# Attention's last two heads projected by token, and the other fourteen heads' sums divided on GpSimd: one change to a two-layer hybrid kernel on one Trainium2 core

## What is computed

```python
x = x + attention(layernorm(x))
# attention, 16 heads of 8 features each
dots = einsum('bhid,bhjd->bhij', q, k) * 8 ** -0.5      # causal mask, ALiBi bias in the second one
attn = softmax(dots, axis=-1)
out  = einsum('bhij,bhjd->bhid', attn, v)               # heads side by side: 128 features
return out @ Wo
```

## Time and profile before

| | |
|---|---|
| median of 3 runs | 2040.76 us (2034.04 to 2040.94) |
| the profiled execution: its time, its span | 2045.5 us, 2043.6 us |
| busy: TensorE, VectorE, ScalarE, GpSimd | 89%, 78%, 58%, 28% of the span |
| mean granted TensorE clock | 0.943 of full |
| first attention: head 15's third chunk copied to `o_sb`, last addition to `x`, start of each | 944.3 us, 988.1 us |
| second attention: the same two | 1939.1 us, 1982.9 us |

### The profile page before, as it was taken

The page is one execution under the profiler, slowest core; times in us unless marked ns, Lnnn a source line. Parts: engine busy times, 40 slices in busy tenths (PEclk is TensorE's granted clock), DMA queues, the critical chain, the costliest instruction groups (busy, mean ns, idle before and its releaser), DMA issues. The chain is left out here.

```text
span 2043.6 us, 47998 instructions
## 1 busy us (share of the span) xinstructions
PE 1823.2 (89%) x18588; PEld 979.6 (48%) x18588; DVE 1584.5 (78%) x3374; ACT 1175.8 (58%) x2363; POOL 563.1 (28%) x528
## 2 busy tenths in 40 slices
PE   6888888999899999998899978888869999999967
PEld 2444454444355555554544434444534555555454
DVE  6899965666889999983555579999568999999545
ACT  4766623222278888885222257755443888888815
POOL 3898920000200000000100048989330000000022
PEclk9999998999699999998799999999887999999969
DMA  5343300310313222211041124443021233322200
GB/s 167 118 140 116 127 1 1 89 51 27 110 31 53 54 56 50 51 27 22 1 81 49 36 63 116 134 122 105 1 73 51 55 56 60 57 56 40 31 4 21
DMA packets 68719, 127.89 MB, mean 63 GB/s; under 512 B 20679, under 2 KB 30932, under 8 KB 67020
## 3 DMA queue, kind: packets, MB, share of 16 engines
q1 hardware_dynamic: 68076, 124.29, 24.4%
q10 hardware_dynamic: 416, 0.54, 0.1%
HBM read 106.17 MB, written 16.84 MB: 60 GB/s over the span
## 5 line engine op out<-in xcount | busy, mean ns | idle before, releaser
L1774 ACT ACTIVATE a_probs<-a_ps_k 128x512 f32<-128x512 f32 (+3 forms) x1280 | 598.6, 546 | 225.1 <-PE a_ps_k L1688 129.9
L1670 PE MATMUL a_ps_q<-a_k_op,a_q_op 84*32 84x512 bf16 (+7 forms) x5120 | 536.3, 366 | 24.7 <-DMA a_k_op<-a_k_parts 9.6
L1834 DVE TENSOR_REDUCE a_maxes<-a_ps_q 128x1 f32<-128x512 f32 x768 | 504.1, 686 | 67.6 <-PE a_ps_q L1670 64.8
L1684 PE MATMUL a_ps_k<-a_q_op,a_k_op 87*32 87x512 bf16 (+7 forms) x5120 | 517.5, 353 | 2.4 <-ACT a_probs L1774 0.8
L1706 PE MATMUL a_ps_o<-a_probs,a_vh 128*32 128x512 f32 (+3 forms) x2752 | 319.3, 509 | 1.1 <-ACT a_probs L1774 0.8
L1670 PEld LDWEIGHTS a_ps_q<-a_k_op,a_q_op 72*32 72x32 bf16 (+1 forms) x5120 | 186.8, 97 | 171.5 <-DVE a_maxes L1834 69.1
L1831 DVE CUSTOM_DVE_ANT_0 a_ps_q<-a_ps_q,all_c_mask_q 128x128 f32<-128x128 f32 (+3 forms) x512 | 248.2, 496 | 4.9 <-PE a_ps_q L1670 3.8
L1684 PEld LDWEIGHTS a_ps_k<-a_q_op,a_k_op 75*32 75x32 bf16 (+1 forms) x5120 | 185.3, 96 | 135.6 <-ACT a_probs L1774 85.1
L1105 ACT ACTIVATE e_silu<-e_psg,all_me_b 128x512 f32<-128x512 f32 x128 | 87.7, 687 | 230.6 <-PE e_psg L1037 230.6
L1914 POOL CAST a_max_parts<-a_neg_max 128x16 bf16<-128x16 f32 x32 | 6.3, 196 | 751.0 <-DVE a_neg_max L1839 751.0
L1188 DVE SCALAR_TENSOR_TENSOR e_mid<-e_psv,all_me_b,e_silu 128x512 f32<-128x512 f32 x128 | 95.7, 749 | 132.2 <-PE e_psv L1039 128.3
(11 more groups left out here) (296 smaller groups left out, 2585.1 us busy)
## 6 DMA issues: line engine op xcount, KB each, us to landing
m0st_c_rows<-m_bc_rows SPq DMA_DIRECT2D x32, 512.0 KB
e_w_rows<-e_comb SPq DMA_DIRECT2D x64, 256.0 KB, 3.3
m1st_c_rows<-m_bc_rows SPq DMA_DIRECT2D x32, 512.0 KB
a_q_op<-a_q_parts SPq DMA_DIRECT2D x30, 288.0 KB
a_k_op<-a_k_parts SPq DMA_DIRECT2D x30, 288.0 KB
a_outputs<-a_o_sb SPq DMA_DIRECT2D x480, 18.0 KB
m0st_b_rows<-m_bc_rows SPq DMA_DIRECT2D x32, 256.0 KB
m1st_b_rows<-m_bc_rows SPq DMA_DIRECT2D x32, 256.0 KB
```

Of the source, the lines that this page charges most:

```text
L1670: last = pe.matmul(ps_q[32 * r:32 * r + 32, use % QB, 0:width], q_op[h % SLOT][0:NR, part(t, r)], k_op[h % SLOT][0:NR, kc * CH:kc * CH + w ...
L1684: last = pe.matmul(ps_k[32 * r:32 * r + 32, b % KB, 0:width], k_op[h % SLOT][:, part(j, r)], q_op[h % SLOT][:, c * CH + first:c * CH + fir ...
L1774: act.activation(probs[:, n % PSLOT, 0:width], ps_k[:, b % KB, 0:width], ACT.Exp).then_inc(exp_done, 1)
L1834: dve.tensor_reduce(found, bank, AX.X, ALU.max).then_inc(q_read, 1)
```

## The change

Four things are done otherwise; FULL = 14 is the number of heads that still go through HBM, LAST = 15.

* Heads 14 and 15 are not stored or moved. When ScalarE has copied a chunk of such a head to `o_sb`, TensorE multiplies each 128-token tile of it, as it is (`direct(h, c)`), with a 128 x 130 matrix `w_direct`: the head's eight rows of `Wo`, repeated for the four groups of partitions, and as column 128 ones at the rows of sums. The result has the token on the partition; its column 128 is that token's sum. VectorE inverts the column and adds `product * inverse` to `x` (`add_direct`). There are eight `direct`s of four matmuls in place of nothing.
* The other 14 heads: GpSimd adds their partial sums in one go (two instructions), VectorE inverts them in one instruction, SyncE stores the inverses to HBM and reads them back spread over the features (`share`, four DMAs that repeat each row eight times); GpSimd adds the four partials (twelve instructions) and multiplies by `share` (four). `spread` and `sel_head` are gone, and so are VectorE's additions and `divide`.
* The projection of those heads, `output(c)`, stays with four matmuls a chunk, now on 112 rows.
* Both use the three banks of `ps_q`, which the stream of maxima has left, and stand inside the loop: `direct(14, 0..3)` from head 14's n = 32 to head 15's n = 4, `output(0..3)` and `direct(15, 0..2)` from n = 12 to n = 32. Only `direct(15, 3)` follows the loop.

```diff
+            def direct(h, c):
+                pe.wait_ge(o_read, NC * h + c + 1)
+                for i in range(2):
+                    use = direct_use[h, c] + i
+                    bank_free(use)
+                    for j in range(2):
+                        last = pe.matmul(ps_q[:, use % QB, j * DW:(j + 1) * DW], o_sb[:, c, tile(2 * i + j)],
+                                         w_direct[:, h - FULL, :], start=True, stop=True)
+                    last.then_inc(q_ready, 1)
 
             def output(c):
-                pe.wait_ge(normed, c + 1)
-                if c >= 2:
-                    pe.wait_ge(added, c - 1)
+                use = output_use[c]
+                pe.wait_ge(divided, c + 1)
+                bank_free(use)
...
@@ ScalarE
-                if h:
+                if h == LAST:
+                    act.wait_ge(q_ready, direct_use[FULL, c] + 2)
+                elif h:
                     act.wait_ge(o_stored[c], h * STORES)
@@ VectorE
+            def add_direct(h, c):
+                for i in range(2):
+                    use = direct_use[h, c] + i
+                    bank = ps_q[:, use % QB, 0:2 * DW].rearrange("p (j f) -> p j f", f=DW)
+                    dve.wait_ge(q_ready, use + 1)
+                    dve.reciprocal(inv_col[:, i, :], bank[:, :, P]).then_inc(col_ready, 1)
+                    if h == LAST:
+                        dve.wait_ge(q_read, output_use[c] + 1)
+                    dve.wait_ge(col_ready, use_number(h, c, i) + 1)
+                    for j in range(2):
+                        xt = x[:, TPC * c + 2 * i + j, :]
+                        last = dve.scalar_tensor_tensor(xt, bank[:, j, 0:P], inv_col[:, i, j:j + 1], xt, ALU.mult, ALU.add)
+                    last.then_inc(q_read, 1)
...
+            dve.wait_ge(summed, 1)
+            dve.reciprocal(inv[:, :, :], inv[:, :, :]).then_inc(inverted, 1)
             for c in range(NC):
-                invert(c)
...
+                add_direct(FULL, c)
+            add_output(0)
+            add_output(1)
+            add_direct(LAST, 0)
+            norm_stats(0)
+            add_output(2)
+            add_output(3)
+            ahead.normalise(dve, 0)
+            add_direct(LAST, 1)
+            norm_stats(1)
+            add_direct(LAST, 2)
+            norm_stats(2)
+            ahead.normalise(dve, 1)
+            ahead.normalise(dve, 2)
+            add_direct(LAST, 3)
@@ GpSimd
+            for h in range(LAST):
                 split_maxima(h)
-                if h + 1 < HEADS:
-                    place(h + 1)
-            pool.wait_ge(k_ready, NK * LAST)
-            pool.wait_ge(o_back, 16 * BACKS * LAST)
+                place(h + 1)
+            pool.wait_ge(k_ready, NK * FULL)
+            pool.wait_ge(o_back, 16 * BACKS * FULL)
+            pool.tensor_tensor(pair[:, :, :, :], sums[:, :, 0:2, :], sums[:, :, 2:4, :], ALU.add).then_inc(paired, 1)
+            pool.wait_ge(paired, 1)
+            pool.tensor_tensor(inv[:, :, :], pair[:, :, 0, :], pair[:, :, 1, :], ALU.add).then_inc(summed, 1)
             for c in range(NC):
...
+                add_upper(c)
+            add_lower(0)
+            split_maxima(LAST)
+            for c in range(NC):
+                if c:
+                    add_lower(c)
+                add_both(c)
+            for c in range(NC):
+                divide(c)
+            for c in range(NC - 1):
                 ahead.power(pool, c)
@@ SyncE
+            load_output(FULL - 1)
+            sp.dma_start(w_direct[:, :, :], dram[tag + "_w_direct"]).then_inc(direct_loaded, 16)
+            load_maxima(LAST)
+            sp.wait_ge(inverted, 1)
+            sp.dma_start(inv_dram.rearrange("c h j t -> (h j) c t"), inv[:, :, :]).then_inc(inv_stored, 16)
+            sp.wait_ge(inv_stored, 16)
+            for c in range(NC):
+                rows = inv_dram[c, :, :, :].rearrange("h j t -> h (j t)").unsqueeze(1)
+                sp.dma_start(share[:, chunk(c)], rows.broadcast_to([FULL, DH, CH])).then_inc(share_loaded[c], 16)
```

More of the change, by code:

```diff
@@ L1503, in attention @@
             ml = Memory(nc, late, tag + "ou")
-            total = ml.sb("total", [P, 2, CH])
-            upper = ml.sb("upper", [P, 2, CH])
-            pair = ml.sb("pair", [P, 2, JT])
-            inv = ml.sb("inv", [P, JT])
-        q_op = [m.sb(f"q_op{s}", [NR_MAX, TOK], BF16) for s in range(SLOT)]
-        k_op = [m.sb(f"k_op{s}", [NR_MAX, TOK], BF16) for s in range(SLOT)]
+            pair = ml.sb("pair", [FULL * SB, NC, 2, JT])
+            inv = ml.sb("inv", [FULL * SB, NC, JT])
+            share = ml.sb("share", [ROWS, TOK])
+        qk_op = [[m.sb(f"{n}_op{s}", [NR_MAX, TOK], BF16) for n in "qk"] for s in range(SLOT)]
+        q_op, k_op = [[pair_[o] for pair_ in qk_op] for o in range(2)]
+        w_direct = m.sb("w_direct", [P, HEADS - FULL, DW])
+        inv_col = m.sb("inv_col", [P, 2, 2])
         vh = [m.sb(f"vh{s}", [P, NT, 32]) for s in range(SLOT)]
@@ L1521, in attention @@
         ps_k = m.ps("ps_k", [P, KB, CH])
-        with ExitStack() as late:
-            ml = Memory(nc, late, tag + "ou")
-            ps_s = ml.ps("ps_s", [P, CH])
-            ps_y = ml.ps("ps_y", [P, 2, CH])
         ps_q = m.ps("ps_q", [P, QB, CH])
@@ L1558, in attention @@
         o_back = m.sem("o_back")
-        last_back = [m.sem(f"last_back{c}") for c in range(NC)]
-        last_sums = [m.sem(f"last_sums{c}") for c in range(NC)]
         paired = m.sem("paired")
@@ L1563, in attention @@
         inverted = m.sem("inverted")
-        spread_ready = m.sem("spread_ready")
+        inv_stored = m.sem("inv_stored")
+        share_loaded = [m.sem(f"share_loaded{c}") for c in range(NC)]
+        direct_loaded = m.sem("direct_loaded")
         upper_ready = m.sem("upper_ready")
@@ L1617, in attention @@
         PIECES = through[NK - 1]
-        def move_sums(eng, c):
-            for r in range(4):
-                eng.dma_start(sums[LAST * SB:(LAST + 1) * SB, c, r, :],
-                              o_sb[32 * r + DH:32 * r + DH + 1, c, :]).then_inc(last_sums[c], 16)
         block = ctx.enter_context(nc.Block())
@@ L1746, in _ @@
                     times_v(h, n)
+                    if h == FULL and n == 32:
+                        pe.wait_ge(direct_loaded, 16)
+                        direct(FULL, 0)
+                    if h == FULL and n == 36:
+                        direct(FULL, 1)
+                    if h == LAST and n == 0:
+                        direct(FULL, 2)
+                    if h == LAST and n == 4:
+                        direct(FULL, 3)
+                    if h == LAST and n == 12:
+                        output(0)
+                    if h == LAST and n == 16:
+                        output(1)
+                        direct(LAST, 0)
+                    if h == LAST and n == 20:
+                        output(2)
                     if h == LAST and n == 24:
-                        pe.wait_ge(q_read, USES)
-                        spread(0)
-                    if h == LAST and n == 28:
-                        output(0)
+                        output(3)
+                        direct(LAST, 1)
                     if h == LAST and n == 32:
-                        spread(1)
-                    if h == LAST and n == 36:
-                        output(1)
-            for c in range(2, NC):
-                spread(c)
-                output(c)
+                        direct(LAST, 2)
+            direct(LAST, 3)
         @block.scalar
@@ L2120, in constants @@
         sel[:, n, n] = 1
-    sel_head = np.zeros((HEADS, SB, SB, HEADS, DH), np.float32)
-    for h in range(HEADS):
-        for b in range(SB):
-            sel_head[h, b, b, h] = 1
     slopes = (2.0 ** (-8.0 / HEADS * (np.arange(HEADS, dtype=np.float32) + 1.0))).astype(np.float32)
```

126 lines of the change are left out of this document (49 added, 77 removed).

## The result

The changed kernel takes **2010.55 us** (median of 4 runs, 2010.23 to 2022.13) against 2040.85 for the kernel before in the same comparison (2034.04 to 2041.42): a ratio of 0.9874, with 95% between 0.985 and 0.9897. Half to two thirds of the forecast gain came: 30 us by the medians, 26 by the ratio, where 46.6 were forecast. The profiled execution took 2010.23 us, its span is 2008.4, its mean clock 0.957 where it was 0.943.

What follows compares the result with a forecast made beforehand. Loop: TensorE and ScalarE nearly full; then 40 us with no engine busy, clock down. Per attention 1947.7 + 8 + 2.1 + 2.5 = 1960.3 against 1983.6: 23.3, twice 46.6; 2040.8 - 46.6 = 1994.2 us, range 1982 to 2012.

Steps and rivals of the forecast that it cites:

- steps on TensorE: In the loop: eleven steps of four fp32 matmuls at 0.95 us, 10.5 in all, partly hidden; 8 us taken, bounds 5 to 10.5.
- the end: After the last copy: direct(15, 3), an inverse, two VectorE instructions and hops, 2.5 us; upper bound 5 for queued normalise(2).
- what there is to win: Loop standstill and the chunks passing one by one behind it: 35.9 us an attention, from 1947.7 to 1983.58.
- `turn` late: TensorE's wait for GpSimd's split of head 15's maxima, behind seven new instructions: 2.1 us late, bounds 0 to 6.
- rival 1: After the attention: the next stage starts at full clock, 5 us an attention more gained, 1984 us; chance 0.12.
- `output(0)` comes free: In head 15's loop: GpSimd's divide(0) ends before TensorE reaches output(0) at about 1938, with 2 us to spare.
- GpSimd beside VectorE: Shared way into SBUF: GpSimd's new additions beside head 14's maxima cost VectorE 0.02 us an instruction, zero in the sum.
- 2, `turn` ten us late: GpSimd's additions hinder the maxima, or head 13's transfers are slow: gain 15.4 us an attention, 2010 us; chance 0.14.
- 3 and 4: 3: output(0) waits for divided, slower than before, 2065, chance 0.03. 4: TensorE still waits at the end, 2029, chance 0.02.
- TensorE's standstills in head 15: Sign of being right: no TensorE standstill over 1 us between head 15's n = 24 and its end.
- chunk 3 follows chunk 2: Sign of being right: head 15's copy of chunk 3 about 14 us after chunk 2 at most, not 22.
- the clock, forecast at 1.00: Sign of being right: clock 1.00 until the last addition at the end of the attention.

Runs made afterwards that it cites:

- kernel of 5: The kernel before the change, with spread and output of chunks 0 and 1 also behind the loop: 2034.47 us, ratio 0.9964.
- kernels of 1 and 4: The change with head 15's split of the maxima behind three GpSimd additions, 2002.46 us; the same plus direct(15, 2) one group sooner, 2000.68 us.
- experiment 3: The change with each of TensorE's twelve steps' matmuls issued twice, 2029.63 us; separately, the change with one matmul instead of four in each output, 2008.12 us.
- the split first: The change with head 15's split of the maxima ahead of all of GpSimd's additions: 2005.25 us, ratio 0.9827.
- the split fourth: The change with head 15's split of the maxima behind two additions of sums and one of partials: 2002.46 us, ratio 0.9815.
- experiment 4: The change with direct(15, 2) after n = 28 instead of n = 32, 2011.98 us; with head 15's split also behind three additions, 2000.68 us.
- experiment 1: The change with head 15's split of the maxima moved up in GpSimd's list: ahead of all additions 2005.25 us, behind three 2002.46 us.
- both edits together: The change with head 15's split behind three of GpSimd's additions and direct(15, 2) one group sooner: 2000.68 us, ratio 0.9787.
- chunk 2 sooner alone: The change with only direct(15, 2) moved, to after n = 28 of head 15 instead of n = 32: 2011.98 us, ratio 0.985.
- the doubled steps: The change with the matmuls of each of TensorE's twelve direct and output steps issued twice: 2029.63 us, ratio 0.9942.

## Why the prediction was wrong

The sign and the mechanism of the gain were right, the size was not: 1994.2 us forecast, 2010.55 measured, at the upper edge of the range of 1982 to 2012. Three terms of the sum were too low: `turn` by 3.5 us, the steps on TensorE by 3.2, the end by 1.75; 0.4 more was to be won than reckoned. That makes the 8 us an attention. Only the steps lie outside the bounds given for them. By the sum's terms, per attention:

| step | forecast | measured, with its source |
|---|---|---|
| what there is to win, from the loop's own pace | 35.9 | 36.3: the free loop takes 28.3, not 28.7 (kernel of 5) |
| steps on TensorE | 8 (5 to 10.5) | 11.2: 39.5 us for the three pieces without a wait (kernels of 1 and 4), less 28.3 |
| `turn` late | 2.1 (0 to 6) | 5.6 (6.05 and 5.15): 4.1 and 3.7 standstill, the rest low clock |
| the end | 2.5 (2 to 5) | 4.25 |
| gain | 23.3 | 15.3 |

**"Eleven steps at 0.95, 8 of 10.5."** Failed, by 3.2 us: I let ScalarE's pace in the loop of before hide a part, and none is hidden. A further four matmuls cost 0.89 (experiment 3), and the eleven steps 11.2, 1.02 each. That the total is even above 10.5 comes from a step that stands alone: after its start at 1910.32 the next instruction starts at 1911.41, 1.09 us later. Where two steps follow each other it is 0.99, as TensorE's timeline shows further on:

```profile
1927.59 1.16 PE L1723 MATMUL a_ps_q<-all_a_wo,a_oT 112*128 112x128 f32 x8
1928.58 1.06 PE L1714 MATMUL a_ps_q<-a_w_direct,a_o_sb 128*128 128x130 f32 x8
1929.57 0.24 PE L1682 MATMUL a_ps_k<-a_q_op,a_k_op 87*32 87x128 bf16 x4
```

The 0.95 was the duration of the row; the next instruction starts there 0.81 us later (1003.71, 1004.52). So the row was no measure of these steps either way: its matmuls have 8 columns, and that 128 or 130 columns fit into the same time is not so here, where four take 1.16 as a row and 0.99 to 1.09 as a distance.

**"The split is 2.1 us late, TensorE stands at `turn`."** Right in kind: it did, released by GpSimd, as forecast. The size failed, by 3.5 us, for two reasons. First, the additions' start, here in the second attention. The store of head 13's last chunk began 14.5 us before the copy of chunk 2 of head 14 (forecast 15.0), its landing took 3.9 us instead of 3.1, and from the first load's issue to the sums 8.1 us passed, not 6.2: 3.2 us later in all than forecast. GpSimd gave back 1.4 of it, with additions at 1.24 instead of 1.36 and a split through in 1.0 instead of 1.4. The 6.2 were read off the DMA share of a window. In the change that share stays at 0.35 or more until 1896, 7.4 us after the issue, and GpSimd starts 0.7 us after that. The load of `w_direct`, issued at 1890.26, runs beside these; the forecast had it cost nothing, and no run leaves it out, so its part in the delay stays open. Second, the sum took the standstill as its own price. The clock that had been seen to fall within 5.15 us of standing still was used against rival 1 and not for this wait; what the piece costs beyond the standstill is 1.5 and 1.9 us.

**"`output(0)` comes free, with 2 us to spare."** Right: no wait on `divided` in either attention. In the second TensorE came there at 1924.26, and the first of the four divisions, 1.24 us each from 1914.96 on, was done at 1916.2. The margin is so large since the wait at `turn` held up TensorE and not GpSimd. With the split first it is gone (1.2 us short); with the split fourth 2.05 and 1.65 us are left, about the 2 that were forecast.

**"The end, 2.5; upper 5 because of `normalise(2)`."** The upper bound named the cause. VectorE normalised chunks 1 and 2 from 1944.73 on and came to the last inverse at 1947.00, 2.5 us after `direct(15, 3)` had begun; with VectorE free (experiment 4) it does so after 1.1 us. That is 1.4 of the 1.75 us too many, in a term whose sum had left out a wait that its own upper bound named; from the inverse on it takes the same 1.66 us.

**GpSimd beside VectorE.** Right: the maxima of head 14 beside the additions took 0.69 us a row of 512, as beside none.

**Rivals.** 1, the next stage at full clock: in the change it wasn't (first row 1.94 us, as before). 2, `turn` ten us late: the number (2010) came out by coincidence. The maxima were not hindered, and of the transfers 2.7 us more came than forecast, not eight. 3 and 4: nothing of them. Right too: TensorE's standstills in head 15 stay under 1 us until `direct(15, 3)`; chunk 3 follows chunk 2 by less than 14 us. Wrong: 4.25 us from the last copy to the last addition, with 4 forecast as the most; the clock, forecast at 1.00 until there, fell at `turn`; and `turn` stood 3.7 and 4.1 us, not about 2.

## What to carry to other kernels

A step that is put into a loop costs the whole distance to the next instruction on the engine that then sets the pace; price it so, and count on no cover from the engine that set the pace before: it gave none here. In a list that runs in order, look at who waits behind an instruction before looking for a faster engine: four small instructions behind the two additions of sums and five of partials cost 5.6 us an attention, and moving them up by four places gave nearly all of it back, as fully as moving the additions to the faster engine did. A new wait on TensorE is priced with what the low clock may take behind it (up to 1.9 us behind 4 here).

## What the runs showed of the hardware

- **The clock can fall after very little.** 1.23 us of standing still was followed by 0.50 in one attention and by 1.00 in the other, of the same execution (experiment 1). Before the stage that follows the second attention 2.82 us did the same: down with both edits together, up with chunk 2 sooner alone; and after 3.03 us it was up with the doubled steps. The first row of that stage, in the first two of these kernels:

```profile
1944.14 1.94 PE L190 MATMUL q_psx<-all_c_ident,all_xn 128*128 128x128 f32 x8 [2.82 <-PEq L86]
```

```profile
1953.81 1.06 PE L190 MATMUL q_psx<-all_c_ident,all_xn 128*128 128x128 f32 x8 [2.82 <-PEq L86]
```

- **Where the next stage began at full clock, it didn't keep it.** With chunk 2 sooner alone the clock was down again 2 us after the stage's first matmul, with TensorE busy most of the time (that kernel's windows, columns as above):

```profile
1954.00:1955.00 1.00, 0.87 (x8) 0.63 (x6) 0.00 (x0) 0.53 (x2) 0.00 (x0) 1.00 0.03 8
1955.00:1956.00 1.00, 0.88 (x3) 0.47 (x3) 0.00 (x0) 0.56 (x2) 0.00 (x0) 0.60 0.00 0
```

  From the last addition to the end of the span it is 59.3 and 59.6 us in the two kernels that began with the clock up, and 59.1 to 60.9 in the eight profiles of the change and its variants that began with it down: no gain can be seen. The 5 us of rival 1 supposed ten us at full clock, which no run had, so they stay untested.
- Left open: why the clock falls behind one of two like waits and not behind the other, how much of the transfers' delay is `w_direct`'s, and what makes the stretches ahead of the attentions differ by some 10 us between executions.
